# A selective-scan kernel: B's diagonal comes by DMA out of a zero image, VectorE adds to y, and the chunk loop is written out

## What is computed

```python
def step(h, inp):                       # one token
    ut, dtt, bt, ct = inp
    dA = jnp.exp(dtt[..., None] * A)
    h = dA * h + (dtt * ut)[..., None] * bt[:, :, None, :]
    y = jnp.einsum('bkdn,bkn->bkd', h, ct)
    return (h, y)
...
ys = ys + Ds.reshape(1, K, D_INNER, 1) * xs        # the skip term
y = ys[:, 0] + col2row(ys[:, 1]) + jnp.flip(ys[:, 2], -1) + col2row(jnp.flip(ys[:, 3], -1))
```

## Time and profile before

| | us |
|---|---|
| median of 3 runs | 31304.53 (31281.53 to 31306.0) |
| the profiled execution, its own time | 31304.37 |
| its span | 31302.4 |
| PE busy in the span | 29091.5 (93%) |
| DVE busy | 27266.5 (87%) |
| POOL busy | 23928.4 (76%) |
| ACT busy | 19120.8 (61%) |

### The profile page before, as it was taken

How to read it: one execution, slowest core, us unless ns; L and a number is a source line. 1 busy time by engine, 2 the same in 40 slices (tenths; PEclk the granted TensorE clock), 3 DMA queues, 4 the chain that set the end, 5 groups by cost and what they waited for, 6 DMA issues and landing times. The chain is left out here.

```text
span 31302.4 us, 684367 instructions
## 1 busy us (share of the span) xinstructions
PE 29091.5 (93%) x247872; PEld 20808.3 (66%) x247872; DVE 27266.5 (87%) x25017; ACT 19120.8 (61%) x38088; POOL 23928.4 (76%) x10772
## 2 busy tenths in 40 slices
PE   9999998998999999899899989989989999998998
PEld 6775775774677577577467757757746775775774
DVE  8987997996898799799689879979968987997996
ACT  5665664664666566466466656656646665664664
POOL 7885985894788598589478869858847885985884
PEclk9999999998999999999899999999989999999998
DMA  1111111121111111112111111112111111111121
GB/s 64 68 61 48 67 66 51 70 72 33 65 67 61 48 67 67 51 70 71 34 66 66 61 49 66 68 50 71 70 34 66 66 61 48 66 68 50 70 71 33
DMA packets 373333, 1881.34 MB, mean 60 GB/s; under 512 B 111332, under 2 KB 115644, under 8 KB 165928
## 3 DMA queue, kind: packets, MB, share of 16 engines
q1 hardware_dynamic: 345448, 1792.34, 16.2%
q10 hardware_dynamic: 24384, 42.48, 0.4%
HBM read 1740.26 MB, written 94.37 MB: 59 GB/s over the span
## 5 line engine op out<-in xcount | busy, mean ns | idle before, releaser
L877 POOL TENSOR_TENSOR regB<-regB,regA 128x1024 f32<-128x1024 f32 x9216 | 21630.3, 2368 | 2844.0 <-ACT carry L707 2815.6
L831 DVE TENSOR_TENSOR_SCAN regB<-regB,carry,ps 128x512 f32<-128x512 f32 x16128 | 19237.2, 1258 | 889.7 <-PE ps L584 345.9
L584 PEld LDWEIGHTS ps<-regA,regB 64*128 64x128 f32 x147456 | 9069.7, 189 | 4928.2 <-DVE regB L831 2723.7
L718 ACT ACTIVATE regB<-regB,a_neg 128x512 f32<-128x512 f32 x18432 | 12192.5, 710 | 30.0 <-issue 30.0
L584 PE MATMUL ps<-regA,regB 64*128 64x128 f32 x147456 | 10844.0, 287 | 797.7 <-DVE regB L831 654.4
L598 PE MATMUL ps<-ident,regB 128*128 128x128 f32 x73728 | 10172.1, 281 | 45.5 <-POOL regB L877 29.5
L598 PEld LDWEIGHTS ps<-ident,regB 128*128 128x128 f32 x73728 | 7978.8, 142 | 1177.7 <-issue 43.9
L707 ACT ACTIVATE carry<-regB 128x2 f32<-128x2 f32 x9216 | 1886.3, 205 | 7922.4 <-DVE regB L831 7869.3
L867 POOL TENSOR_TENSOR regB<-regB,u 128x512 f32<-128x512 f32 x1152 | 1622.1, 1408 | 2065.0 <-DVE regB L801 2065.0
L831 DVE TENSOR_TENSOR_SCAN regB<-regB,ps 128x512 f32<-128x512 f32 x2304 | 2621.4, 1199 | 173.4 <-PE ps L584 171.9
L812 DVE TENSOR_TENSOR regA<-fold,ps 128x1024 f32<-128x1024 f32 x1536 | 1808.7, 1199 | 366.8 <-PE ps L558 366.8
(11 more groups left out here) (83 smaller groups left out, 15885.7 us busy)
## 6 DMA issues: line engine op xcount, KB each, us to landing
regA<-xd SPq DMA_DIRECT2D x1536, 1024.0 KB, 4.8
regA<-x_in SPq DMA_DIRECT2D x16, 1536.0 KB, 14.6
x_keep<-regA SPq DMA_DIRECT2D x8, 3072.0 KB, 18.8
regA<-x_keep SPq DMA_DIRECT2D x16, 1536.0 KB, 16.2
regB<-xd SPq DMA_DIRECT2D x128, 192.0 KB
xd<-regB ACTq DMA_DIRECT2D x96, 256.0 KB
xd<-regB ACTq DMA_DIRECT2D x192, 88.0 KB
regB<-w_in_in SPq DMA_DIRECT2D x28, 576.0 KB, 4.9
```

Of the source, the lines that this page charges most:

```text
L584: mm = nc.tensor.matmul(ps[:, 2 * (g % 2) + i, q * 2 * RT:(q + 1) * 2 * RT], dtuT[at, up, q, :], diag[at, cp, q, g], start=True, stop=True)
L718: nc.scalar.activation(decays[:, g % 2, s], dt[:, up, :], ACT.Exp, scale=a_neg[:, c[0], d, 2 * g + s:2 * g + s + 1]).then_inc(a_made, 1)
L831: nc.vector.tensor_tensor_scan(ring[:, g % RING, s, way], decays[:, g % 2, s, way], b[:, s, way], 0.0 if begun else carry[:, d, at:at + 1] ...
L877: nc.gpsimd.tensor_tensor(ring[:, g % RING], ring[:, g % RING], c_all[:, g], ALU.mult).then_inc(g_made, 1)
```

## The change

**B's diagonal.** B's rows of a chunk are stored a second time, to a DRAM tensor `b`, in runs of 64 tokens (store_b). A DRAM tensor `eye` of two images (one for even and one for odd chunks), 128 rows x 4096 floats each, is filled with zeros once, at the start. In channel block 0, step 4 (ACT_B), ACT issues two DMAs (spread) that copy the 8192 values of B of the next chunk one by one onto the diagonals of the 64 x 64 blocks of that image; the zeros round them stay. SP waits for both and loads the whole image, 128 x 16 KB, into `diag` (load_diag), between the loads of dt and of C. load_b, turn_b, make_diag and the `fold` constant are gone.

**The layout of diag.** Its last dimension is now (s t), one state after the other, and the matmuls of inputs write their columns into the PSUM bank with a jump of two, so that the bank holds what it held before.

**y.** start_y and keep_y are gone. turn_y moves from step 5 to 4 and starts the bank itself. At step 6 DVE reads the bank and writes y_acc (add_y): u times the summed skip weight plus the bank for k = 0, y_acc plus the bank for the others.

**The loop.** chunks writes out all 8 chunks of a direction, with constants in place of registers.

The diff, cut to its core:

```diff
@@ build @@
+        b_dram = [nc.dram_tensor(f"b_{l}", (K, NCH, NS * T), F32).ap() for l in range(3)]
+        eye_dram = nc.dram_tensor("eye", (2, P * EYE + RT), F32).ap()
...
+                sp.wait_ge(zero_set, 1)
+                for c in range(2):
+                    sp.dma_start(eye_dram[c, 0:P * EYE].rearrange("(p x) -> p x", p=P), zeros).then_inc(zeroed, 16)
+                sp.wait_ge(zeroed, 32)
...
+                nc.vector.memset(zeros, 0.0).then_inc(zero_set, 1)
@@ scan, chunks @@
-                    step(chunk_of(k, 0, 0), before, chunk_of(k, 1, 0), 0)
-                    with eng.Fori(0, NCH // 2 - 1) as j:
-                        c = [chunk_of(k, j * 2 + i, j + i // 2) for i in range(4)]
-                        step(c[1], c[0], c[2], 1)
-                        step(c[2], c[1], c[3], 0)
-                    step(chunk_of(k, NCH - 1, NCH // 2 - 1), chunk_of(k, NCH - 2, NCH // 2 - 1), after, 1)
+                    c = [chunk_of(k, n, n // 2) for n in range(NCH)]
+                    for n in range(NCH):
+                        step(c[n], c[n - 1] if n else before, c[n + 1] if n + 1 < NCH else after, n % 2)
...
+            def store_b(eng, k, n, rows, sem):
+
+                eng.dma_start(b_dram[l][k, n].rearrange("(a n r) -> n a r", n=NS, r=RT),
+                              rows.rearrange("n (a r) -> n a r", r=RT)).then_inc(sem, 16)
@@ scan, SP @@
+                    def load_diag(c, cp):
+                        S = c[3]
+                        sp.wait_ge(spread_b, (S + 1) * ROWS * 16)
+
+                        wait(sp, b_made, (S - 1) * NDB * PAIRS)
+                        sp.dma_start(diag[:, cp].rearrange("p q g t -> p (q g t)"),
+                                     eye_dram[cp, 0:P * EYE].rearrange("(p x) -> p x", p=P)).then_inc(diag_loaded, 16)
...
-                            sp.wait_ge(bt_mm, after[3])
                             if after[0]:
 
-                                sp.wait_ge(xd_stored, (after[3] - NCH + 1) * 16)
-                            load_b(after)
+                                sp.wait_ge(xd_stored, (after[3] - NCH + 1) * 32)
                             load_dts(after)
+                            load_diag(after, 1 - par)
@@ scan, PE @@
-                                mm = nc.tensor.matmul(ps[:, 2 * (g % 2) + i, q * 2 * RT:(q + 1) * 2 * RT],
+                                b = ps[:, 2 * (g % 2) + i, q * 2 * RT:(q + 1) * 2 * RT]
+                                mm = nc.tensor.matmul(b.rearrange("p (t s) -> p s t", s=2),
                                                       dtuT[at, up, q, :], diag[at, cp, q, g],
                                                       start=True, stop=True)
...
-                                if g == PE_SKIP and (old := behind(this, before, d, 0, PAIRS)):
-                                    start_y(old[0], old[1], par_of(old[0], par, this, old[1]))
@@ scan, ACT @@
+                    def spread(c, cp):
+
+                        k, n, _, S = c
+
+                        wait(act, spread_b, S * ROWS * 16)
+                        if k == 0:
+                            act.wait_ge(xd_pre, (PRE_FREE + n + 1) * 32)
+                        else:
+                            act.wait_ge(xd_stored, (S - NCH + 1) * 32)
+                        rows = b_dram[l][k, n].rearrange("(i a r) -> i a r", i=ROWS, r=RT)
+                        for i in range(ROWS):
+                            onto = eye_dram[cp, i * RT * EYE:i * RT * EYE + RT * (EYE + 1)].rearrange(
+                                "(r x) -> r x", x=EYE + 1)[:, 0:EYE].rearrange("r (a b) -> a r b", b=RT)
+                            act.dma_start(onto[:, :, 0:1], rows[i].rearrange("a (r o) -> a r o", o=1),
+                                          allow_slow_non_contiguous=True).then_inc(spread_b, 16)
...
                                     act.dma_start(xd_of(k + 1, n), xd_out[0:M]).then_inc(xd_stored, 16)
+                                    store_b(act, k + 1, n, xd_out[R:R + NS], xd_stored)
+                                if d == 0 and after and g == ACT_B:
+                                    spread(after, 1 - par)
...
-                                if g == ACT_Y and (old := behind(this, before, d, 0, PAIRS)):
-                                    keep_y(old[0], old[1], par_of(old[0], par, this, old[1]))
@@ scan, DVE @@
+                    def add_y(c, d, up):
+
+                        k, n, _, S = c
+                        dve.wait_ge(y_mm, unit(c, d) + 1)
+                        y, got = in_order(y_acc, k, d, n), as_chunk(ps[:, Y_BANK + up, :], k)
+                        if k == 0:
+                            nc.vector.scalar_tensor_tensor(y, in_order(u, k, d, n), dsum[:, d:d + 1], got,
+                                                           ALU.mult, ALU.add).then_inc(y_kept, 1)
+                        else:
+
+                            dve.wait_ge(y_kept, unit(c, d) - NDB + 1)
+                            nc.vector.tensor_tensor(y, y, got, ALU.add).then_inc(y_kept, 1)
```

More of the change, by code:

```diff
@@ L551, in project_dt @@
                                          dts[0:R + 1], start=True, stop=True).then_inc(z_mm, 1)
-                    def turn_b(c):
-                        S = c[3]
-                        pe.wait_ge(brow_loaded, (S + 1) * ROWS * 16)
-                        for q in range(QS):
-                            mm = nc.tensor.matmul(ps[:, T_BANK, q * NS:(q + 1) * NS],
-                                                  brow[:, q * P:(q + 1) * P], ident[0:NS, 0:NS],
-                                                  start=True, stop=True)
-                        mm.then_inc(bt_mm, 1)
                     def turn_dtu(c, d):
@@ L634, in _ @@
                     pe.wait_ge(xd_copied, COPIED)
-                    turn_b(first)
                     project_dt(first, 0)
-                    pe.wait_ge(diag_made, QS)
                     turn_dtu(first, 0)
@@ L647, in step @@
                                     sums(*old, par_of(old[0], par, this, old[1]))
-                                if d == 1 and g == PE_BT and after:
-                                    pe.wait_ge(dtT_made, unit(this, 1) + 1)
-                                    turn_b(after)
                                 if nxt and g == PE_Z:
@@ L833, in scans @@
                                 0.0 if begun else carry[:, d, at:at + 1], ALU.mult, ALU.add).then_inc(scanned, 1)
+                    def add_y(c, d, up):
[8 more added lines that the diff above has]
+                            nc.vector.tensor_tensor(y, y, got, ALU.add).then_inc(y_kept, 1)
                     nc.vector.memset(dts[:], 1.0).then_inc(ones_set, 1)
                     first = chunk_of(0, 0, 0)
-                    for q in range(QS):
-                        make_diag(first, q, 0)
                     make_dt(first, 0, 0)
@@ L848, in step @@
                                     make_dt(*nxt, par_of(nxt[0], par, this, nxt[1]))
-                                if d == 1 and after:
-                                    for q in range(QS):
-                                        if g == DVE_DIAG[q]:
-                                            make_diag(after, q, 1 - par)
+                                if g == DVE_Y and (old := behind(this, before, d, 0, PAIRS)):
+                                    add_y(old[0], old[1], par_of(old[0], par, this, old[1]))
                     chunks(dve, step)
+                    add_y(LAST, NDB - 1, NDB % 2)
                 @block.gpsimd
```

102 lines of the change are left out of this document (31 added, 71 removed).

## The result

The changed kernel takes 30300.97 us (median of 4 runs, 30289.26 to 30303.74), the kernel before 31299.97 us beside it (31281.53 to 31306.0): a ratio of 0.9683, with a 95% interval of 0.9669 to 0.9697. It is 1.0 ms faster, where the prediction said 0.8 ms slower. Its profiled execution has a span of 30299.0 us.

What follows compares the result with a forecast made beforehand. DVE was taken to set the scans' pace, with PE close behind. 31.30 - 1.06 (engine work and loop) + 1.77 (single-float DMAs) + 0.12 (scan heads, zeros) = 32.13 ms; forecast 32100 us, range 30300 to 36900.

Steps and rivals of the forecast that it cites:

- the floats are cheap: Rival on the single-float DMAs: at 14 to 20 ns a packet ACT's stall is nearly covered, 30.4 ms; chance 0.30.
- step 6: ACT's two single-float DMAs: at 35 ns a packet ACT stands 6.3 us, 2.5 covered; +4.6 us a chunk, +1.77 ms.
- make_diag goes: DVE no longer builds B's diagonal: four operations of 1.12 us, 4.5 us of DVE saved a chunk.
- add_y, +2.6 us of DVE: DVE adds y three times a chunk, 0.61 us each plus 0.49 in odd directions; bounds 1.8 and 3.3 us.
- PE -5.4 us: PE loses start_y (about 4.3 us a chunk) and turn_b (1.1), falling from 65.9 to 60.5 us, below DVE's 62.9.
- the rival on PSUM: Inputs' matmuls writing PSUM with a jump get slower: 36.9 ms, or 34 to 35 at half the factor; chance 0.24.
- The scan's pace is DVE's: Inside the scans DVE sets the pace, with PE some 1 us of work a chunk more and no room behind it.
- The loop, -0.33 ms: Writing out the chunk loop removes DVE's idle time behind 96 backward jumps, 3.4 us each, 0.85 us a chunk.
- keep_y off ACT, nothing: ACT loses three copies a chunk of 0.57 or 1.06 us; worth nothing, since ACT waits for DVE in most steps.
- The turning point: Where the forecast's sign turns: ACT may stand some 4.5 us for the single-float DMAs, 25 ns a packet.
- Data and image hidden: Both halves' floats take 18 us and the 2 MB image 10 us, ending near the chunk's middle, so they cost nothing.
- Head of each scan: At each scan's start the image load delays C's first piece: 8 us a scan, 0.10 ms, plus 0.02 once for zeros.

Runs made afterwards that it cites:

- the third DMA: The changed kernel with a third DMA of 4096 single floats behind the two, into an image nobody reads: 33479.3 us (one run).

## Why the prediction was wrong, step by step

The rival "the floats are cheap", 30.4 ms at a chance of 0.30, is what happened. The step that failed is step 6: the price of a 4-byte packet, put at 35 ns, and with it the 6.3 us that ACT was to stand. The lower end of the stated range, 30300 us, had been put there for this rival, and the time came out 1 us above it.

1. *make_diag goes, -4.5 us of DVE.* Right: 4.2 (1610 / 384, from the page of the written-out loop to that of loop and diagonal).
2. *add_y, +2.6 us of DVE, bounds 1.8 and 3.3.* Right: 2.3. In direction 1 it stands 1.21 us ahead of the next operation (1002.80 to 1004.01), 0.58 in direction 2 (1305.80 to 1306.38); 1.10 and 0.61 were said.
3. *PE -5.4 us.* Right in size: 5.0, of it 1.05 for turn_b, 3.5 for y's part (4.3 were said) and 0.45 with the loop, which had no term. The 1.02 us for sums are right for most steps, but the earlier trace rows has 0.93 (33.64 to 34.57); and no row gives the 65.1 us from which the rival on PSUM takes PE's room. "The scan's pace is DVE's" was misread. With the loop written out it is true of direction 3, and for less than half of the 4.2 us in direction 1; in direction 0 PE was busy 65.1 of 66.0 us, and taking 4.1 us from DVE brought 0.2. So the terms of steps 1 and 2, -1.9 us a chunk or -0.73 ms, gave 0.53 in the chunks of the scans, from the profile with the loop alone to the one without the spread (25288 and 24756 us). Nor do the parts simply add: y's part costs 0.52 ms on top of the loop alone, and 0.04 on top of loop and diagonal.
4. *The loop, -0.33 ms.* Under-sized: 0.59 ms, 6.2 us for each of the 96 jumps. (The rows gave 3.7 us, and the sum went on with 3.4.) The earlier trace rows are one turn, in direction 1. The trace of before had worse ones in direction 3, which the prediction did not read:

```profile
1961.98 2.45 DVE L831 TENSOR_TENSOR_SCAN regB<-regB,carry,ps 128x512 f32<-128x512 f32 x2 [7.00 <-PE ps L584]
...
2103.00 2.45 DVE L831 TENSOR_TENSOR_SCAN regB<-regB,carry,ps 128x512 f32<-128x512 f32 x2 [7.79 <-PE ps L584]
```

5. *keep_y off ACT, nothing.* Not tested apart; ACT waits for DVE's scans 6784.7 us in the changed kernel, so nothing speaks against it. The second store of B has no term: ACT waits for it 204.0 us in 67 waits, where it had waited 51.4 us for the one store before; what of that reaches DVE is not shown.
6. *The spread, +1.77 ms.* It costs 0.07. The count held for the second issue (197 packets an engine against 180), the place held, and the cover was larger (4.3 us against 2.5, without dt's two operations). What failed is the duration: ACT stood 2.70 us and not 6.3. Between 14 ns (small, into SBUF) and 95 ns (2 KB, into DRAM) the geometric mean, 35 ns, was taken, when in the 95 ns nearly all was the 2 KB. The size decided, not the target: 4 bytes into DRAM took 9.8 ns of engine time, and 13.7 ns in elapsed time while ACT waits. The turning point that the prediction worked out, 25 ns, was right next to the later rate of 26 ns, but in the changed kernel that part of the queue holds nobody. This is a margin that the prediction didn't know of, and the third DMA used it up. A term on which the sign hangs was carried by a mean between two unlike rows.
7. *Data and image hidden.* Right in effect: with all that the spread does gone, 0.07 ms was left to gain, and the view of waits has no wait of PE for the image. Both halves took some 12 us instead of 18 (1056.65 until after 1068), and the image landed in 7.7 us (median) instead of 10.
8. *Head of each scan, +0.10 ms, and 0.02 once.* By the profiles all that lies outside the chunks of the scans grew by 50 us in the changed kernel and by 70 without the spread (5404, 5454 and 5473 us): 0.05 to 0.07 for 0.12.

Without the spread the kernel is 1.07 ms under before; steps 1 to 5 and 8 had said 0.94. That the sum without the floats was good to 0.13 ms is partly luck, by errors of opposite sign: the loop gave 0.26 ms more than said, the work off DVE 0.20 less, and the heads cost some 0.05 less. And one term was 24 times too large. The rival on PSUM, at a chance of 0.24, drew the range up to 36900 us and was nothing.

## What to carry to other kernels

A packet's cost goes first by its size: price small descriptors by the nearest row of that size, and where the forecast's sign hangs on the guess, say the case of the nearest row first. A DMA issue that is held costs only what its cover leaves: count the packets the issuer must wait for, not those of its own transfer, and move the second issue some steps down. Look by stage (here by direction) which engine leads before adding up one engine's terms, and where a stall repeats, read several of its instances.

## What the runs showed of the hardware

- Single floats from DRAM to DRAM: 9.8 ns of DMA engine time a packet; in elapsed time 13.7 ns for the first 200 on each engine, the start included, and about 26 ns from there on, with an uneven pace. The issue of 4096 floats takes 0.52 us on an empty queue, 2.70 us behind one such DMA and 8.69 us behind two.
- PE's float32 matmuls write PSUM with a jump of 2 floats at the same pitch as in one run, 1.09 us for 16 of them. A matmul of 512 moving columns has two rows in the trace; each takes 1026 ns when the columns are read from SBUF with a jump of 64 floats, and 594 when they are read in runs of 8 floats, with that jump on PSUM's side. VectorE's add went from a mean of 1079 to 663 ns the same way. The Trainium skill (Advanced Engine Details and Errata, Memory Cachelines) has SBUF in lines of 16 bytes, with a penalty where each access meets another line; that agrees, for both engines.
- A turn of a hardware loop over two chunks cost 6.2 us on average, with DVE idle up to 7.8 us at one.
